# A two-layer graph network on one core: an earlier-reading first part, transfers of 128 rows, and the first layer's one-hot on ScalarE

## The chip, the core and the metric

The program runs on one core of a Trainium2 chip. Five engines work side by side and meet only at semaphores: TensorE (PE in the profile; its weight loads are PEld), VectorE (DVE), ScalarE (ACT), GpSimd (POOL) and SyncE (SP, which only issues transfers). ACT and POOL issue transfers too. Each engine takes its instructions strictly in the order in which they are written. The metric is device time in microseconds, and lower is better.

## The reference

Two message-passing layers over 12,500 nodes of 160 features (64 scalars and 32 vectors of three) and 200,000 edges. Cut to what matters:

```python
edge_index = stack([src, dst])                 # dst is sorted, src is not
for layer in (0, 1):
    xj   = x[dst]                              # gather, one row per edge
    msg  = tensor_product(xj, edge_attr) + linear(xj)      # 160 values per edge
    agg  = segment_sum(msg, src, num_segments=12500)       # scatter-add by src
    upd  = tensor_product(x, agg) + linear(x)  # bilinear: u, v -> w, 64*64*64 and more
    x    = layernorm(x + (x + upd))
return x
```

The first tensor product is linear in `xj` once the four edge attributes are given; the second is bilinear in the node's features and its sum.

## The kernel before, in words

**Tiles.** The nodes are cut into 100 tiles of `HM` = 125. The edges, in the order of `dst`, are cut into 98 chunks of 16 blocks of 128, and each chunk into two units of 8 blocks (196 units). For each node a row of 5 x 160 values (`table`) is stored in memory, from which every message of an edge that reads the node is a combination. A unit reads windows of 25 nodes of the table (`win`), builds a picking matrix for its edges (`pick_e`, on DVE, `select`), turns it on PE (`turn_pick`, into `s_ps`), ACT copies it out (`pick_out`), PE multiplies it with the window (`messages`, into `m_ps` and in the first part also `node_ps`), ACT copies the messages into `pay` (`pay_out`), and POOL writes them with eight indirect transfers a unit to the slots that belong to the edge's `src` tile (`scatter`). A node tile later reads its 17 x 128 slots (`msgs`), and PE sums them with a one-hot matrix of the slots' local node numbers (`onehot`, `sum_edges`).

**Three stages.** After a setup (loading and turning the edge lists, first tables) comes the first part, `chunk_sweep`: for each chunk layer 0's table tile eight ahead, both units of messages, and the sorting that gives each edge its slot. The sorting is `count` on PE (five small bf16 matmuls, twice a unit: `count(g, 0)` and `count(g, 1)`), `rank_unit` on DVE (a chain of 16 dependent operations that ends by raising `placed`) and the copy of the slot numbers on ACT. Then `step_sweep`, layer 0's node steps: step t sums the edges of tile t, runs the bilinear update of tile t - 1 (`bilinear(0)` to `(5)`, `turn_q`, `linear`), makes the layer-1 table rows of tile t - 2, and does chunk t - 7 of layer 1's messages. Last `node_sweep`, layer 1's node steps, with no messages. The middle of each sweep is a loop of two bodies on every engine.

**What sets the order.** Nothing but the order of the code on each engine, written out by hand, and the buffers: one `m_ps` and one `node_ps` bank, one `s_ps` bank, two `pick_n`, four `pay` and four `slot` buffers. In the first part `addressed` on ACT waits for `placed` of its own unit before it copies the slots, and `pay_out` of the same unit stands behind it. In a node step ACT begins with `where(0)`, `out(0, 0)` (the copy of `pick_n` for the first unit), `paid(0, 0)`, and ends with `turned_y` (copies of `ys_t`, `a_t`, `v_t`, for the next `bilinear(0)`) and `paid(1, 3)`; PE's step begins `bilinear(0)`, `turn(0, 0)`, `bilinear(1)`, `message(0, 0)`, and ends `turn_y`, `message(1, 3)`.

**The one-hot.** In layer 0 DVE makes it with one comparison over 128 x 2125, as the last thing of its step, for the next tile. In layer 1 ACT makes it: 17 `Square` activations of (node number - local number), a wait, and one `Relu(1 - 2 x)` over 128 x 2125.

**Transfers.** `slots` are cleared ahead of the scatter by ACT (`fill`, 22 rows of each of the 100 tiles per chunk, source one row of zeros 168 wide), and `spill_sums` by `clear`, once in two chunks. SP stores tables and results in 125 rows, and loads `x`, `spill_sums` in 125 rows and the windows in 125 (`WROWS` = 5 x 25).

Of the kernel before, what the change touches and what calls it, by code (L numbers as in the profile page):

```python
# [6 lines left out]
ALU = mybir.AluOpType  # L7
# [6 lines left out]
P = 128  # L14
# [3 lines left out]
HM = 125  # L18
# [60 lines left out]
def build(nc, x, src, dst, attr, weights, out):  # L79
# [35 lines left out]
    table = [nc.dram_tensor(f"table{layer}", [EDGE + N + EDGE, CHANNELS * D], F32).ap() for layer in range(2)]  # L115
# [4 lines left out]
    with ExitStack() as whole:  # L120
# [26 lines left out]
        zero = sb("zero", [P, ROW])  # L147
# [175 lines left out]
        def fill_ranks(eng, layer, r0, ranks, filled):  # L323

            rows = slots[layer][0:SLOTS, :].rearrange("(t r) c -> t r c", r=CAP)
            eng.dma_start(rows[:, r0:r0 + ranks, :] if isinstance(r0, int) else rows[:, bass.ds(r0, ranks), :],
                          zero[0:NT, :].unsqueeze(1).broadcast_to([NT, ranks, ROW])).then_inc(filled, 16)

        @block.sync
        def _(sp):  # L330
# [18 lines left out]

            def load_table_x(k):  # L350
# [3 lines left out]
                sp.dma_start(tx[b][0:HM, :], x[bass.ds(m * HM, HM), :]).then_inc(tx_in[b], 16)  # L354
# [52 lines left out]
            def load_windows(layer, k):  # L407
# [3 lines left out]
                if isinstance(c, int):  # L411
                    for m in (last_tile(c) - 1, last_tile(c)):
                        if m >= 0:
                            sp.wait_ge(s["t_stored"][m % 2], 16 * (m // 2) + 16)
                else:
                    sp.wait_ge(s["t_stored"][0], 16 * (ck + (1 if cb == 0 else 2)) + 16)
                    carry()
                    sp.wait_ge(s["t_stored"][1], 16 * (ck + 1) + 16)
                    carry()
                for hh in range(2):  # L420
# [4 lines left out]
                    for p in range(QUADS):  # L425
                        rows = table[layer][bass.ds(at[p], EDGE + WIN), :]
                        both = bass.AP(rows.tensor, rows.offset, [[D, WROWS], [EDGE * CHANNELS * D, 2], [1, D]], runtime_checks=rows.runtime_checks)
                        sp.dma_start(win[q][0:WROWS, 2 * p:2 * p + 2, :], both).then_inc(s["win_in"][q], 16)  # L428

            def store_table(layer, k):  # L430
# [1080 lines left out]
```

## Time and profile before

| | us |
|---|---|
| median of three runs | 8602.44 (8588.28 to 8614.11) |
| profiled execution | 8569.22, its span 8567.5 |
| setup, to the first scatter | 215.87 |
| first part, first scatter to last | 215.87 to 2865.9 |
| layer 0's node steps and the tail of the scatters | 2892 to 6024 |
| layer 1's node steps | 6024 to 8567.5 |
| busy over the span: PE, DVE, POOL, ACT | 79%, 82%, 52%, 33% |
| mean granted TensorE clock | 0.875 |

Read it by stages, since the shares differ: in the first part no engine is busy for more than about 60%, in layer 0's node steps PE and DVE are both busy for 96 to 97%, in layer 1's steps DVE for 96%. Granted clock 1.0 is 2.4 GHz, and 0.5 is 1.2 GHz; a mean between them is a mix of stretches at the one and at the other. POOL's busy time leaves out some 0.30 us between two scatters, in which it prepares the next.

### The profile page before, as it was taken

The page shows a single profiled execution, that of the slowest core. Times are in us where ns is not written, and L with a number is a line of the kernel's source. Part 1 is how long each engine was busy: PE and PEld are TensorE (multiplying, and loading weights), DVE is VectorE, ACT ScalarE, POOL GpSimd, SP SyncE. Part 2 cuts the span into 40 slices and gives each one's busy share as a digit, 9 for nine tenths or more (in the row PEclk, how much of TensorE's full clock was granted, in tenths as well). Part 3 has the DMA queues.
Part 4 walks back from the last instruction along what each step waited for, and adds up shares of the span by engine and source line. Part 5 has one row for each costly group of instructions (what it writes and reads, how often), then busy time and mean ns, then how long its engine had stood idle before and what let it go on. Part 6 is the DMA issues. An engine that isn't in the chain of part 4 may idle for free.

```text
span 8567.5 us, 139797 instructions
## 1 busy us (share of the span) xinstructions
PE 6727.2 (79%) x38863; PEld 5022.4 (59%) x38863; DVE 6998.7 (82%) x9199; ACT 2869.7 (33%) x9562; POOL 4429.7 (52%) x3371
## 2 busy tenths in 40 slices
PE   2666656666566699999999999997788888888888
PEld 1444444444444467777777777775556566666665
DVE  2655555555556799999999999996899999999999
ACT  1222222222222123333333333333344444444443
POOL 0655555555556357777777777777222222222222
PEclk5777777777777799999999999998899999999999
DMA  5555555555555256666666666664221212121211
GB/s 144 160 159 155 156 154 161 157 157 155 160 159 144 83 162 186 186 185 188 187 188 188 188 186 186 185 188 124 75 71 65 70 64 71 64 71 64 71 64 50
DMA packets 984231, 1163.06 MB, mean 136 GB/s; under 512 B 74878, under 2 KB 878173, under 8 KB 958553
## 3 DMA queue, kind: packets, MB, share of 16 engines
q10 hardware_dynamic: 460746, 590.81, 23.3%
q0 software_dynamic: 154640, 281.49, 11.6%
q1 hardware_dynamic: 368767, 289.81, 11.5%
q8 instruction: 39, 0.64, 0.0%
q14 instruction: 39, 0.32, 0.0%
HBM read 480.47 MB, written 681.31 MB: 136 GB/s over the span
## 4 chain that ended last, share of the span: by engine, by line
PE 39%; DVE 23%; issue 12%; DMA 8%; SPq 8%; ACT 5%; ACTq 4%; DVEq 1%; POOL 0%; POOLq 0%
PE prods_ps L1105 7%; PE turn_ps L1129 7%; PE node_ps L1138 6%; PE m_ps L1042 6%; DMA table<-tab 6%; DVE work L898 4%; SPq L428 3%; PE s_ps L1025 3%; PE node_ps L1042 3%; DVE pick L757 2%; DVE pick L755 2%; DVE rank L758 2%; PE node_ps L1150 2%; ACTq L1218 2%; DVE upd L904 2%
## 5 line engine op out<-in xcount | busy, mean ns | idle before, releaser
L544 POOL DMA_INDIRECT slots<-pay,slot x3136 | 3273.3, 1044 | 1727.9 <-ACT pay L1295 931.7
L601 POOL TENSOR_TENSOR q<-xt,yv 125x3072 f32<-125x3072 f32 x200 | 1130.4, 5652 | 2298.4 <-PE turn_ps L1129 2270.9
L1042 PE MATMUL m_ps<-win,pick_n 125*128 125x160 f32 x4704 | 1068.5, 355 | 784.0 <-ACT pay L1295 769.9
L1106 PE MATMUL prods_ps<-w_bil,ys_t 64*125 64x512 f32 x2400 | 1465.7, 708 | 0.0
L1042 PEld LDWEIGHTS m_ps<-win,pick_n 125*128 125x128 f32 x4704 | 769.5, 213 | 1113.2 <-ACT pay L1295 894.9
L898 DVE TENSOR_TENSOR work<-prods_ps,yv 125x1024 f32<-125x1024 f32 x1200 | 1392.9, 1217 | 11.2
L904 DVE TENSOR_REDUCE upd<-work 125x48 f32<-125x3072 f32 x400 | 1341.3, 3353 | 13.6
L1129 PEld LDWEIGHTS turn_ps<-ident,q 125*128 125x128 f32 x9600 | 1110.4, 192 | 175.6 <-issue 153.0
L1129 PE MATMUL turn_ps<-ident,q 125*128 125x125 f32 x9600 | 1162.4, 278 | 16.6 <-ACT q_t L1373 16.4
L1105 PE MATMUL prods_ps<-w_bil,a_t 64*125 64x512 f32 x1600 | 1016.9, 741 | 176.1 <-ACT v_t L1402 115.2
L882 DVE TENSOR_TENSOR work<-prods_ps,xt 125x1024 f32<-125x1024 f32 x800 | 964.1, 1219 | 149.7 <-PE prods_ps L1106 135.0
L1138 PEld LDWEIGHTS node_ps<-msgs,onehot 128*125 128x125 f32 x6800 | 931.0, 188 | 169.0 <-issue 169.0
L1138 PE MATMUL node_ps<-msgs,onehot 128*125 128x160 f32 x6800 | 979.7, 303 | 17.6 <-ACT onehot L1449 11.0
L886 DVE TENSOR_REDUCE upd<-work 125x16 f32<-125x1024 f32 x800 | 950.8, 1209 | 0.0
L1025 PE MATMUL s_ps<-ident,pick_e 128*125 128x128 f32 x3136 | 646.2, 341 | 285.6 <-ACT pick_n L1277 276.8
L1025 PEld LDWEIGHTS s_ps<-ident,pick_e 128*125 128x125 f32 x3136 | 564.0, 247 | 377.6 <-issue 367.5
L754 DVE TENSOR_TENSOR before<-before,prods_ps 128x100 f32<-128x100 f32 x392 | 100.3, 256 | 830.1 <-PE prods_ps L1013 830.1
L1277 ACT COPY pick_n<-s_ps 125x512 f32<-125x512 f32 x784 | 459.7, 586 | 768.1 <-PE s_ps L1025 458.9
L1295 ACT COPY pay<-m_ps 128x320 f32<-128x320 f32 x1176 | 506.5, 431 | 483.9 <-PE m_ps L1042 475.2
L1105 PEld LDWEIGHTS prods_ps<-w_bil,a_t 64*125 64x125 f32 x1600 | 287.4, 214 | 594.3 <-DVE work L882 288.3
L1105 PE MATMUL prods_ps<-w_bil,ys_t 64*125 64x512 f32 x800 | 448.7, 641 | 109.8 <-DVE work L882 109.8
L1446 ACT ACTIVATE onehot<-node_iota,msgs 128x125 f32<-128x125 f32 x1700 | 503.9, 395 | 54.4 <-POOLq L588 54.4
(216 smaller groups left out, 8479.8 us busy)
## 6 DMA issues: line engine op xcount, KB each, us to landing
msgs<-slots ACTq DMA_DIRECT2D x200, 1428.0 KB, 6.5
slots<-zero ACTq DMA_DIRECT2D x183, 1443.8 KB
win<-table SPq DMA_DIRECT2D x784, 156.2 KB
table<-tab SPq DMA_DIRECT2D x200, 390.6 KB
slots<-pay,slot POOLq DMA_INDIRECT x3136, 5.5
spill_sums<-zero_rows ACTq DMA_DIRECT2D x88, 180.0 KB, 9.5
spill_in<-spill_sums SPq DMA_DIRECT2D x200, 78.1 KB
rec<-edge_recs SPq DMA_DIRECT2D x196, 64.0 KB, 8.6
```

Source lines behind the costliest of these rows:

```text
L544: g.indirect_dma_start(out=slots[layer][:, :], out_offset=bass.IndirectOffsetOnAxis(ap=slot[q][:, j:j + 1], axis=0), in_=pay[q][:, j, :], ...
L601: g.tensor_tensor(q3[0:HM, :].rearrange("p (i u v) -> p i u v", i=3, u=V), xt[nb][0:HM, S:D].rearrange("p (u i) -> p i u", i=3).unsqueeze( ...
L882: ve.tensor_tensor(third(r), prods_ps[r % 2][0:HM, :].rearrange("p (w u) -> p w u", u=S), X[:, 0:S].unsqueeze(1).broadcast_to([HM, ROUND / ...
L886: ve.tensor_reduce(upd[0:HM, ROUND // S * (r - 1):ROUND // S * r], third(r - 1), AX_X, ALU.add).then_inc(s["upd"], 1)
L898: ve.tensor_tensor(wk[:, i, :, :].rearrange("p w (h k) -> p h w k", h=2), prods_ps[r % 2][0:HM, :].rearrange("p (h w k) -> p h w k", h=2, ...
L904: ve.tensor_reduce(upd1[:, :, w0:w0 + ROUND // KV], wk, AX_X, ALU.add).then_inc(s["upd"], 1)
L1025: mm = te.transpose(s_ps[0:WROWS, P * j:P * j + P], pick_e[hh][:, UB // 2 * part + j, :, :].rearrange("p n c -> p (n c)"), ident[:, :])
L1042: mm = te.matmul(to[:, D * j:D * j + D], pick_n[hh][0:WROWS, P * (2 * p + j):P * (2 * p + j) + P], win[q][0:WROWS, p, :], start=True, stop ...
L1105: te.matmul(prods_ps[r % 2][0:HM, 0:512], upper, w.bil[0:S, 512 * r:512 * r + 512], start=True, stop=True)
L1106: te.matmul(prods_ps[r % 2][0:HM, 512:1024], ys_t[S:P, :], w.bil[S:P, 512 * r:512 * r + 512], start=True, stop=True).then_inc(s["prods"], 1)
L1129: mm = te.matmul(turn_ps[:, HM * j:HM * j + HM], q3[0:HM, o:o + P], idn, start=(i == 0), stop=(i == 2))
L1138: te.matmul(node_ps[0:HM, 0:D], onehot[:, j, :], msgs[b][:, j, 0:D], start=(j == 0), stop=False)
```

## The change

Three things are changed at once.

1. **The first part's order.** On PE `count(g, 1)` stands behind the first `turn_pick` of its unit, and `count` for half 0 of the next unit stands ahead of `messages` 2 of this one. On ACT `addressed` is cut in two: `located` (the local numbers, no wait for `placed`) stays, and `slotted` (the slot numbers) comes one unit later, behind `pay_out` 0. POOL's scatter waits for both.
2. **Transfers.** Loads of `x`, of spilled sums and of windows take 128 rows instead of 125 (tables get rows of padding for it). Stores of 125 rows are cut into 112 and 13. The clearing of the slots is cut into 96 tiles and 4, and its source is now 11 rows of zeros, so that one contiguous piece has 1848 values instead of 168. Semaphore counts follow.
3. **The first layer's one-hot** leaves DVE. ACT makes it as in layer 1, in both layers behind `paid(1, 3)`, the last thing of the step; the first one comes after the spill's end.

```diff
 def fill_ranks(eng, layer, r0, ranks, filled):
     rows = slots[layer][0:SLOTS, :].rearrange("(t r) c -> t r c", r=CAP)
-    eng.dma_start(rows[:, r0:r0 + ranks, :] if isinstance(r0, int) else rows[:, bass.ds(r0, ranks), :],
-                  zero[0:NT, :].unsqueeze(1).broadcast_to([NT, ranks, ROW])).then_inc(filled, 16)
+    halves = 2 - ranks % 2
+    cols = ranks // halves * ROW
+    for t0, t1 in ((0, NTP), (NTP, NT)):
+        to = rows[t0:t1, r0:r0 + ranks, :] if isinstance(r0, int) else rows[t0:t1, bass.ds(r0, ranks), :]
+        eng.dma_start(to.rearrange("t (a r) c -> t a (r c)", a=halves),
+                      zero[t0:t1, 0:cols].unsqueeze(1).broadcast_to([t1 - t0, halves, cols])).then_inc(filled, 16)
...
+def put_tile(to, r0, frm, done):
+    sp.dma_start(to[bass.ds(r0, PART), :], frm[0:PART, :]).then_inc(done, 16)
+    sp.dma_start(to[bass.ds(r0 + PART, HM - PART), :], frm[PART:HM, :]).then_inc(done, 16)
...
-    both = bass.AP(rows.tensor, rows.offset, [[D, WROWS], [EDGE * CHANNELS * D, 2], [1, D]], runtime_checks=rows.runtime_checks)
-    sp.dma_start(win[q][0:WROWS, 2 * p:2 * p + 2, :], both).then_inc(s["win_in"][q], 16)
+    both = bass.AP(rows.tensor, rows.offset, [[D, P], [EDGE * CHANNELS * D, 2], [1, D]], runtime_checks=rows.runtime_checks)
+    sp.dma_start(win[q][:, 2 * p:2 * p + 2, :], both).then_inc(s["win_in"][q], 16)
...
@@ tensor engine, first part, chunk(k), one unit @@
     turn_pick(0, k, hh, 0)
-    count(4 * c + 2 * hh, 0)
+    count(4 * c + 2 * hh + 1, 1)
     turn_pick(0, k, hh, 1)
-    count(4 * c + 2 * hh + 1, 1)
     messages(0, k, hh, 0, both)
...
+    if hh == 0 or within(c, 0, NCH - 1):
+        count(4 * c + 2 * hh + 2, 0)
     messages(0, k, hh, 2, both)
...
@@ scalar engine, first part, chunk(k), one unit @@
     pick_out(0, k, hh, 1)
-    addressed(0, k, hh)
+    located(0, k, hh)
     pay_out(0, k, hh, 0, both)
+    if hh == 1 or within(c, 1, NCH):
+        slotted(0, k if hh else earlier(k), 1 - hh)
...
@@ scalar engine, end of node_step @@
     turned_y()
-    if layer == 1 and within(t, 0, NT - 1):
-        one_hot(later(k))
     paid(1, 3)
+    if within(t, 0, NT - 1):
+        one_hot(layer, later(k))
...
@@ vector engine, end of node_step @@
-    if layer == 0 and within(t, 0, NT - 1):
-        one_hot(later(k))
```

PE in the loop of the first part, first unit of a body, **before**; `prods_ps` is the bank of `count`, the two rows to `s_ps` are `turn_pick`:

```order
L1025 MATMUL s_ps<-ident,pick_e 125x128 [waits pick_out_l0,picked_l0]
...
L1011 MATMUL prods_ps<-bucket_onehot,after_bf 128x500 [waits hot]
...
L1025 MATMUL s_ps<-ident,pick_e 125x128 [waits pick_out_l0,picked_l0]
...
L1011 MATMUL prods_ps<-bucket_onehot,after_bf 128x500 [waits hot]
...
L1042 MATMUL m_ps<-win,pick_n 128x160 [waits pay_out_l0]
...
L1042 MATMUL node_ps<-win,pick_n 128x160 [waits pay_out_l0]
...
L985 MATMUL turn_ps<-ident,tx 96x125 [waits tx_in0]
...
L1042 MATMUL m_ps<-win,pick_n 128x160 [waits pay_out_l0]
...
L1042 MATMUL node_ps<-win,pick_n 128x160 [waits pay_out_l0]
```

The same place **now**:

```order
L1033 MATMUL s_ps<-ident,pick_e 125x128 [waits pick_out_l0,picked_l0]
...
L1019 MATMUL prods_ps<-bucket_onehot,after_bf 128x500 [waits hot]
...
L1033 MATMUL s_ps<-ident,pick_e 125x128 [waits pick_out_l0]
...
L1050 MATMUL m_ps<-win,pick_n 128x160 [waits pay_out_l0]
...
L1050 MATMUL node_ps<-win,pick_n 128x160 [waits pay_out_l0]
...
L993 MATMUL turn_ps<-ident,tx 96x125 [waits tx_in0]
...
L1019 MATMUL prods_ps<-bucket_onehot,after_bf 128x500 [waits hot]
...
L1050 MATMUL m_ps<-win,pick_n 128x160 [waits pay_out_l0]
...
L1050 MATMUL node_ps<-win,pick_n 128x160 [waits pay_out_l0]
```

The second count now is the one for the next unit, and it stands ahead of the two messages that wait for `pay_out` of this unit; the first is this unit's second half.

ACT at the same place **before** (`slot` and the second `pay` row are `addressed`, the rows to `pay` from a bank are `pay_out`):

```order
L1277 COPY pick_n<-s_ps 125x512 [waits pick_turned_l0]
L1284 ISA
L1286 REGISTER_ALU [waits placed]
L1287 ISA [waits scattered0_l0]
L1287 COPY slot<-slot_all 128x8
L1288 ISA
L1289 COPY pay<-rec 128x8 [waits rec_in0_l0]
L1294 REGISTER_ALU
L1295 COPY pay<-m_ps 128x2x160 [waits msg_l0]
...
L1295 COPY pay<-node_ps 128x2x160 [waits msg_l0]
```

and **now**:

```order
L1287 COPY pick_n<-s_ps 125x512 [waits pick_turned_l0]
L1294 REGISTER_ALU
L1295 ISA [waits scattered0_l0]
L1296 COPY pay<-rec 128x8 [waits rec_in0_l0]
L1308 REGISTER_ALU
L1309 COPY pay<-m_ps 128x2x160 [waits msg_l0]
L1302 ISA
L1303 ISA [waits placed]
L1303 COPY slot<-slot_all 128x8
...
L1309 COPY pay<-node_ps 128x2x160 [waits msg_l0]
```

The wait for `placed` moved behind the first copy of messages, and it is for the unit before.

ACT over the end of one layer-0 node step and the start of the next, **before**:

```order
L1402 COPY v_t<-turn_ps 96x125
L1295 COPY pay<-m_ps 128x2x160 [waits msg_l1]
L290 UNCONDITIONAL_BRANCH
L290 ISA
L1287 ISA [waits scattered0_l1]
L1287 COPY slot<-slot_all 128x8
L1288 ISA
L1289 COPY pay<-rec 128x8 [waits rec_in0_l1]
L1273 ISA
L1275 ISA [waits pick_turned_l1]
L1277 COPY pick_n<-s_ps 125x512 [waits msg_l1]
```

and **now**:

```order
L1420 COPY v_t<-turn_ps 96x125
L1309 COPY pay<-m_ps 128x2x160 [waits msg_l1]
L1464 ACTIVATE onehot<-node_iota,msgs 128x125 [waits edges_done_l0,msgs_in1_l0]
L1464 ACTIVATE onehot<-node_iota,msgs 128x125 x16
L1467 ACTIVATE onehot<-onehot,ones_f 128x2125 [waits squared]
L294 UNCONDITIONAL_BRANCH
L294 ISA
L1295 ISA [waits scattered0_l1]
L1296 COPY pay<-rec 128x8 [waits rec_in0_l1]
L1303 ISA
L1303 COPY slot<-slot_all 128x8
...
L1287 COPY pick_n<-s_ps 125x512 [waits msg_l1]
```

Eighteen activations now stand between the last `pay` copy of a step and the first `pick_n` copy of the next.

## Rows read from the trace of the kernel before

**Rows 1.** Engines by stage: window, busy us (instructions), granted clock, DMA share, GB/s

```profile
core 0: us, PE busy (x) PEld busy (x) DVE busy (x) ACT busy (x) POOL busy (x), PEclk, DMA share, GB/s
450.00:2800.00 2350.00, 1419.90 (x6355) 1115.33 (x6356) 1374.36 (x3619) 609.61 (x2046) 1365.53 (x1379) 0.73 0.56 156
3150.00:5856.00 2706.00, 2597.93 (x16520) 1959.24 (x16518) 2621.70 (x2413) 970.00 (x3493) 2096.97 (x1517) 1.00 0.64 186
6118.00:8500.00 2382.00, 2031.19 (x12357) 1447.18 (x12356) 2287.05 (x2078) 1016.30 (x3112) 514.55 (x94) 0.92 0.19 67
```

**Rows 2.** Waits in 450 to 2800: who waited for whom, us, times, longest

```profile
ACT slot L1287 <- DVEq L773: 961.2, 173, 6.3
DVE before L754 <- PE prods_ps L1013: 748.7, 212, 9.0
...
ACT pick_n L1277 <- issue: 287.5, 41, 10.3
```

**Rows 3.** Timeline, first part: start, us, engine, line, operation, idle before and its ender

```profile
2336.09 0.20 ACT L1287 COPY slot<-slot_all 128x8 int32 x1 [5.68 <-DVEq L773]
...
2336.77 1.43 PE L1042 MATMUL m_ps<-win,pick_n 125*128 125x160 f32 x4 [3.78 <-ACT pay L1295]
...
2340.02 5.63 ACTq L1218 DMA_DIRECT2D spill_sums<-zero_rows  x1
...
2345.84 2.22 ACTq L326 DMA_DIRECT2D slots<-zero  x1
...
2348.58 0.58 ACT L1277 COPY pick_n<-s_ps 125x512 f32<-125x512 f32 x1 [8.72 <-issue]
...
2351.78 0.26 DVE L754 TENSOR_TENSOR before<-before,prods_ps 128x100 f32<-128x100 f32 x1 [7.43 <-PE prods_ps L1013]
```

**Rows 4.** Groups of instructions, 450 to 2800: the scatters, busy, mean ns, idle before

```profile
L544 POOL DMA_INDIRECT slots<-pay,slot x1379 | 1366.5, 991 | 984.8 <-ACT pay L1295 684.5 <-issue 300.3
```

**Rows 5.** Timeline, POOL: the first and the last scatter of the first part

```profile
215.87 1.46 POOL L544 DMA_INDIRECT slots<-pay,slot  x1 [157.69 <-ACT pay L1295]
...
2864.94 0.96 POOL L544 DMA_INDIRECT slots<-pay,slot  x1 [0.30 <-issue]
```

**Rows 6.** Issue on SP's queue, ns min/median/max: windows (450 to 2800), records (120 to 2800)

```profile
L428 SPq DMA_DIRECT2D win<-table x347: 277/1363/10717, 446.5 to 2790.1; - x174
...
L404 SPq DMA_DIRECT2D rec<-edge_recs x97: 365/366/6085, 196.2 to 2785.4; - x97
```

**Rows 7.** The chain that ended last, in the setup: start, us, what

```profile
14.26 6.08 SPq L354
...
158.92 7.27 DMA tx<-x
```

**Rows 8.** Timeline of one layer-0 node step, its handovers between PE and ACT

```profile
4671.34 0.27 PE L1159 MATMUL turn_ps<-ident,yx 125*96 125x125 f32 x1
...
4672.25 0.43 ACT L1295 COPY pay<-m_ps 128x320 f32<-128x320 f32 x1
...
4674.36 0.58 ACT L1277 COPY pick_n<-s_ps 125x512 f32<-125x512 f32 x1 [1.48 <-PE s_ps L1025]
...
4675.23 0.81 PE L1042 MATMUL m_ps<-win,pick_n 125*128 125x160 f32 x4
...
4701.34 0.27 PE L1159 MATMUL turn_ps<-ident,yx 125*96 125x125 f32 x1
```

**Rows 9.** Waits in 3600 to 5800 (73 node steps)

```profile
DVE work L882 <- PE prods_ps L1106: 43.4, 86, 1.0
```

**Rows 10.** Timeline, DVE: the one-hot at the end of steps 6 and 98

```profile
3066.74 2.37 DVE L858 TENSOR_TENSOR onehot<-msgs,node_iota 128x2125 f32<-128x2125 f32 x1
...
5855.23 2.37 DVE L858 TENSOR_TENSOR onehot<-msgs,node_iota 128x2125 f32<-128x2125 f32 x1
```

**Rows 11.** Timeline, ACT in a layer-1 step: its one-hot

```profile
7200.71 5.04 ACT L1446 ACTIVATE onehot<-node_iota,msgs 128x125 f32<-128x125 f32 x17
7205.79 2.07 ACT L1449 ACTIVATE onehot<-onehot,ones_f 128x2125 f32<-128x2125 f32 x1
```

More of the change, by code:

```diff
@@ L41 @@
 STRIP = 22
+HALF = STRIP // 2
 AHEAD = 5
+PART = 112
+NTP = 96
 LAG = 7
@@ L348, in _, with rows_of @@
             load_piece(so.src_i[1], so.dst_i[1], so.attr[1], 1, 1, piece_in[1])
+            def rows_of(t):
+                return P if within(t, 0, NT - 1) else HM
+            def put_tile(to, r0, frm, done):
+                sp.dma_start(to[bass.ds(r0, PART), :], frm[0:PART, :]).then_inc(done, 16)
+                sp.dma_start(to[bass.ds(r0 + PART, HM - PART), :], frm[PART:HM, :]).then_inc(done, 16)
             def load_table_x(k):
@@ L537, in scatter @@
                 g.wait_ge(s["located"], 2 * c + hh + 1)
+                g.wait_ge(s["slotted"], 2 * c + hh + 1)
                 if within(c, 2 - 2 * layer, STRIPS[layer]):
-                    g.wait_ge(s["filled"][cb], 16 * ck + 16 * layer)
+                    g.wait_ge(s["filled"][cb], 32 * ck + 32 * layer)
                 for p in range(PAIRS):
@@ L850, in spill @@
                 ve.wait_ge(s["sp_done"], 1)
-            def one_hot(k):
-                t, half, b = k
-                s = LS[0]
-                ve.wait_ge(s["msgs_in"][b], 16 * half + 16)
-                if within(t, 1, NT):
-                    ve.wait_ge(s["edges_done"], t)
-                ve.tensor_tensor(onehot[:, :, :], msgs[b][:, :, LOCAL:LOCAL + 1].broadcast_to([P, BLOCKS, HM]),
-                                 node_iota[:, :].unsqueeze(1).broadcast_to([P, BLOCKS, HM]), ALU.is_equal).then_inc(s["hot"], 1)
             def node_step(layer, k, chunk):
@@ L930, in normalise @@
                 if within(n, 2, NT):
-                    ve.wait_ge(s["stored"][b], 16 * half)
+                    ve.wait_ge(s["stored"][b], 32 * half)
                     if layer == 0:
@@ L1066, in _ @@
                     first_table((m, m // 2, m % 2), part)
+            count(0, 0)
             chunk_sweep(te, chunk)
@@ L1210, in fill @@
                 if within(c, 4 - 2 * layer, NCH):
-                    ac.wait_ge(filled, 16 * ck - 16 + 16 * layer)
+                    ac.wait_ge(filled, 32 * ck - 32 + 32 * layer)
                 fill_ranks(ac, layer, r0, min(STRIP, CAP - r0) if isinstance(c, int) else STRIP, filled)
@@ L1277, in pick_out, with located, slotted @@
                 ac.copy(pick_n[hh][0:WROWS, o:o + UB // 2 * P], s_ps[0:WROWS, 0:UB // 2 * P]).then_inc(s["pick_out"], 1)
-            def addressed(layer, k, hh):
+            def located(layer, k, hh):
                 c, ck, cb = k
                 s, q = LS[layer], 2 * cb + hh
+                if within(c, 2, NCH):
+                    ac.wait_ge(s["scattered"][q], 16 * UB * ck)
+                ac.wait_ge(s["rec_in"][cb], 16 * ck + 16)
+                ac.copy(pay[q][:, :, LOCAL:LOCAL + 1], rec[cb][:, UB * hh:UB * hh + UB, LOC:LOC + 1]).then_inc(s["located"], 1)
+            def slotted(layer, k, hh):
+                c, ck, cb = k
                 if layer == 0:
                     ac.wait_ge(placed, 2 * c + hh + 1)
-                if within(c, 2, NCH):
-                    ac.wait_ge(s["scattered"][q], 16 * UB * ck)
-                ac.copy(slot[q][:, :], slot_all[:, bass.ds(2 * UB * c + UB * hh, UB)])
-                ac.wait_ge(s["rec_in"][cb], 16 * ck + 16)
-                ac.copy(pay[q][:, :, LOCAL:LOCAL + 1], rec[cb][:, UB * hh:UB * hh + UB, LOC:LOC + 1]).then_inc(s["located"], 1)
+                ac.copy(slot[2 * cb + hh][:, :], slot_all[:, bass.ds(2 * UB * c + UB * hh, UB)]).then_inc(LS[layer]["slotted"], 1)
             def pay_out(layer, k, hh, p, banks):
@@ L1326, in _ @@
             chunk_sweep(ac, chunk)
+            slotted(0, (NCH - 1, NCH // 2 - 1, 1), 1)
             def deviation(layer, n):
@@ L1351, in where @@
                     if units:
-                        addressed(1, chunk, hh)
+                        located(1, chunk, hh)
+                        slotted(1, chunk, hh)
                 def features():
@@ L1460, in _ @@
             ac.wait_ge(LS[0]["sp_done"], 1)
+            one_hot(0, (0, 0, 0))
             step_sweep(ac, lambda k, chunk: node_step(0, k, chunk))
```

55 lines of the change are left out of this document (28 added, 27 removed).

## The prediction

> **What bounds the kernel now.** I read the engines by stage first, then in each stage the waits, the timeline of one period, and the queue's issue times.
>
> By stage [rows 1] the reader is to see two quite different stages. In 450 to 2800 (the first part) PE and DVE are busy for 60% and 58%, the granted clock is 0.73. In 3150 to 5856 (layer 0's node steps) PE is busy for 96% and DVE for 97% at clock 1.0. In layer 1's steps DVE is busy for 96%.
>
> *First part.* The window holds 1379 scatters, so 172.4 units of 8, a unit each 13.6 us. The waits [rows 2] form a ring: ACT waits for `placed` (961 us), DVE for PE's counts (749 us). The timeline [rows 3] shows why: `slot` ends a wait of 5.68 us, only then is `pay` copied, only then can PE go on (3.78 us idle), and PE's next count stands behind that. Beside the ring, once in a loop body (41 times, 7.0 us each) ACT stands in the issue of its own transfers (5.63 and 2.22 us), and DVE then waits 7.43 us. From the first to the last scatter the stage takes 215.87 to 2865.9 [rows 5], 2650 us, 13.52 us for each of the 196 units.
>
> *Layer 0's node steps.* From step 6's one-hot to step 98's [rows 10] are 92 steps in 2788.5 us, 30.3 us each. Both PE and DVE are full, so it matters who waits. DVE waits for PE's products 86 times, 43 us in 73 steps [rows 9]; no wait of PE for DVE stands among the long ones there, and one undisturbed step measures 4671.34 to 4701.34, 30.0 us, on PE's last transpose [rows 8]. I read PE's stream, with its short handovers to ACT, as the limit.
>
> **The change part by part.**
>
> *Order of the first part.* The ring is cut: messages no longer wait for this unit's `placed`, and the next unit's first count is ahead of them. What is late next is the busiest engine by itself. DVE: 13.63 less 749/172.4 = 4.34 is 9.3 us a unit. PE: 1420/172.4 = 8.2 us, at a clock of 0.73. POOL: 0.99 us a scatter [rows 4] and 0.30 between two [rows 5], so 8 x 1.30 = 10.4 us. POOL is the longest; four `pay` buffers let ACT run ahead of it. I take 10.6, with 0.2 for the waits at a unit's start; the lower end is 10.3, the upper is unknown, since an undiscovered second ring can hold anything up to the present 13.5, and I keep 12.0 for the range. 196 x (13.52 - 10.6) = 572 us saved. The first scatter waits half a unit more for `slotted`: 7 us.
>
> *Transfers.* ACT's 7.0 us a body are counted in the 572 already; they must go for it. A clearing DMA goes from 2200 pieces of 672 bytes to 200 of 7392. An issue of a window takes 1.36 us in the middle and up to 10.7, one of the records, which have 128 partitions, 0.37 in the middle [rows 6]: 125-row issues stand in a full queue. The Trainium skill ("DMA: Bandwidth & Descriptors", section "Why a DMA increments its semaphore by 16 and not by 1") says that a hardware-queue transfer is spread over the largest number up to 16 that divides its outer size: 5 for 125 rows, 10 for 100, all 16 for 128, 112 and 96. By that rule the queue was full because a third of the engines carried it, and the stall goes; if only the amount of bytes filled it, the stall stays, since the bytes do. The rows agree with the rule so far. Cost of the added issues (the 13-row and 4-tile ones): 0.3 us each on SP and ACT, under slack in both stages. In the setup SP stood 6.08 us in one small load and 7.27 us for another to land [rows 7]; between nothing and 60 us can go from there, and I take 40, an estimate: several such landings follow one another there, and the weight loads stand behind the same queue. In layer 0's steps the transfers lie beside a full PE: 0.3 us a step at most (30.3 against 30.0).
>
> *The one-hot off DVE.* 2.37 us a step [rows 10]. In steps 7 to 98 PE is the limit, so DVE only idles: 0. In steps 0 to 6, without messages, up to 7 x 2.4 = 17; I take 15, less 5 for the first one-hot, which now takes 7.15 us before step 0. 10 saved.
>
> *The one-hot onto ACT.* 17 Squares take 5.04 us and the Relu ends 7.15 us after their start [rows 11]. It starts when the last `pay` is copied, 4672.68 [rows 8], and ends at 4679.8. Only then can ACT copy `slot` (0.2) and `pick_n` (0.58): ready at 4680.6. PE's `m_ps` stands behind that copy, and began at 4675.23. So PE is held by 5.4 us. From there to its last transpose (4675.23 to 4701.61) PE has 26.4 us of work in one piece, and what follows on ACT is again v_t, `pay` and the one-hot: the delay returns in every step and nothing takes it back. Behind `pick_n` on ACT stand all `pay` copies and the deviation, behind PE's message stand `bilinear(2)` to `(5)`, for which DVE waits; DVE's 27.6 us fit.
>
> The hole costs PE its clock too. In the first part four matmuls of `m_ps` took 1.43 us after 3.78 us idle [rows 3], and 0.81 us in a full step [rows 8]. Layer 1's steps (94 in 2382 us, 25.3 each) run at clock 0.92 [rows 1], so 0.16 of them, 4.1 us, at 1.2 GHz: up to 2.0 us lost where PE sets the pace. I take 1.8; the ends are 0 and 2.6. The Trainium skill ("TensorE: Matmul & The Clock Gate", section "HAM oscillation — how this bites in real kernels") says that each wait between bursts throttles the next one, and puts the penalty at half the throttled time; by it the step is 37.2, without it 35.4. The two m_ps rows agree with it.
>
> A step is 30.0 + 5.4 + 1.8 = 37.2 us, 6.9 more than 30.3, in 93 steps (7 to 99): 642 us lost. Layer 1's steps keep their order, and their one-hot its place: 0. The scatters' tail after step 99 is POOL's and stays.
>
> *Sum.* -572 + 7 - 40 - 10 + 642 = +27 us on the profiled 8569.2. The median of the runs lies 33 us above that execution; with the same distance after, 8602.4 + 27 = 8629.
>
> **The rivals.**
>
> *No clock loss.* If PE keeps 2.4 GHz through the hole, a step costs 35.4 and the loss is 93 x 5.1 = 474: 8629 - 168 = 8461, faster. For it: layer 1 has stretches at 2.4 GHz through shorter gaps; against it: the first part's rows after 3.78 us. It ends on the other side; it decides from 1.5 us a step downward.
>
> *A second ring in the first part.* The counts, the two single banks and `slotted` still tie DVE, PE and ACT together; at 1.2 GHz PE's own 8.2 us would become more. At 11.6 us a unit the gain is 376: 8825. For it: 4 of 5 us of the saving rest on nothing else appearing; against it: four buffers and DVE's 9.3. A queue that stays full has the same size: 7.0/4 = 1.75 us a unit, mostly hidden by POOL.
>
> *ACT's one-hot is hidden.* If PE had other work in the hole or the 1.48 us that ACT waited [rows 8] were more, the steps stay at 30: 8629 - 642 = 7987. Against it: PE's order is fixed.
>
> *The first part does not move.* If POOL's start, not the ring, paced it: 9200. Against it: its 685 us of waiting for `pay` [rows 4].
>
> **How the numbers follow.** The forecast 0.53, no clock loss 0.17, the second ring 0.22, the hidden one-hot 0.04, no gain 0.04. About 0.3% (26 us) is what a measurement of this kernel can tell from no change; the forecast, +27, lies on that line, and its own range is 8560 to 8710, from 10.4 to 10.9 us a unit and 36.6 to 37.6 us a step. Of its 0.53, 0.08 fall below -26, 0.22 within, 0.23 above. Faster: 0.17 + 0.04 + 0.08 = 0.29. Same: 0.22 + 0.02 from the neighbours = 0.24. Slower: 0.47. The range leaves out the last two cases and the far ends of the rings: 8455 to 8830.
>
> **What would show it.** The one-hot rows on ACT, 7.1 us in each layer-0 step, and behind them a PE wait at `m_ps` for ACT of 5 us or more; the distance of PE's last transposes near 37 us; the stage's clock below 1.0, near 0.92; DVE idle for 8 us in a step. In the first part scatters without gaps, 10.4 to 10.8 us a unit, DVE's wait for counts under 1.5 us a unit, ACT's wait for issue gone, window issues near 0.4 us. Wrong it is if the unit stays above 11.2 us, or if PE's wait at `m_ps` in the steps is under 4 us.

## The result and the profile after

The changed kernel takes 8634.0 us (median of 5 runs, 8627.95 to 8637.45). The kernel before, run beside it, takes 8595.9 (5 runs, 8569.8 to 8614.1). The ratio is 1.0046, with a 95% interval of 1.0025 to 1.0067: about 38 us slower. The forecast was 8629.

Two changes of 600 us stand behind that small number. Stage by stage, in the two profiled executions (8569.2 and 8637.4 us):

| stretch | before | after | difference | forecast |
|---|---|---|---|---|
| to the first scatter | 215.9 | 188.1 | -28 | -33 |
| first part, first to last scatter | 2649.1 | 2072.1 | -577 | -572 |
| from there to layer 0's step 7 | 225.4 | 232.3 | +7 | -10 |
| steps 7 to 99 | 2786.2 | 3453.5 | +667 | +642 |
| after step 99, the scatters' tail and layer 1 | 2691.0 | 2689.6 | -1 | 0 |

(The steps' places are POOL's products, one a step: 3090.4, 5876.6 before; 2492.6, 5946.1 after.) On the profiled executions that is +68 us, where the sum said +27. The medians differ by only 38: the profiled execution of before lies 27 us below the median of its five runs (and under the fastest of them, 8569.81), that of after 3 above its own. The forecast had added 33 us for the first of these distances and kept them for after. So the hit on 8629 owes 36 of the 41 us by which the sum was off to which executions were profiled, and that is luck; the two large terms are right to 1% and 4%.

By stage (columns as in [rows 1]):

```profile
450.00:2200.00 1750.00, 1169.67 (x6112) 916.33 (x6112) 1314.77 (x3488) 586.10 (x1957) 1346.60 (x1324) 0.82 0.67 200
2550.00:5900.00 3350.00, 2788.92 (x16511) 2092.85 (x16511) 2421.06 (x2323) 1575.52 (x5083) 1920.98 (x1520) 0.91 0.50 151
6200.00:8560.00 2360.00, 2019.36 (x12262) 1437.73 (x12262) 2267.45 (x2059) 1007.99 (x3094) 514.54 (x94) 0.92 0.20 68
```

In the first part every engine is busier than in [rows 1], POOL most: 1346.6 us and, beside it, the 0.30 us between scatters. In layer 0's steps PE fell from 96% to 83% and DVE from 97% to 72%: no engine is full any more, as when engines wait for each other in turn. Layer 1 is unchanged.

The first and last scatter of the first part, on POOL's timeline, answer to [rows 5]:

```profile
188.13 1.40 POOL L564 DMA_INDIRECT slots<-pay,slot  x1 [175.19 <-issue]
...
2260.26 0.96 POOL L564 DMA_INDIRECT slots<-pay,slot  x1 [0.30 <-issue]
```

The group of the scatters in 450 to 2200 answers to [rows 4]:

```profile
L564 POOL DMA_INDIRECT slots<-pay,slot x1324 | 1347.7, 1018 | 403.6 <-issue 366.4 <-ACT pay L1309 27.7 <-ACT slot L1303 5.5
```

The waits there answer to [rows 2]:

```profile
ACT pay L1296 <- DMA slots<-pay,slot: 542.4, 107, 7.8
POOL slots L564 <- issue: 366.4, 1202, 0.3
PE m_ps L1050 <- ACT pay L1309: 354.4, 91, 5.8
...
DVE before L774 <- PE prods_ps L1021: 211.1, 82, 5.8
```

2072.1 / 196 = 10.57 us a unit, and 8 x (1.018 + 0.30) = 10.54: POOL works without a pause, and its wait for `pay` went from 684.5 us in a window of 2350 [rows 4] to 27.7 in 1750. Now ACT waits for POOL's transfers to free a buffer of `pay` (542 us), and PE's waits at `m_ps` hang on that. Long waits of the two engines that feed POOL are therefore no loss: they are back pressure, that is, the waits of engines that are ahead of the one that sets the pace.

One layer-0 step of the changed kernel, its handovers between ACT and PE (compare [rows 8]):

```profile
4677.38 0.27 PE L1169 MATMUL turn_ps<-ident,yx 125*96 125x125 f32 x1
...
4678.69 5.04 ACT L1464 ACTIVATE onehot<-node_iota,msgs 128x125 f32<-128x125 f32 x17
...
4683.76 2.07 ACT L1467 ACTIVATE onehot<-onehot,ones_f 128x2125 f32<-128x2125 f32 x1
...
4685.93 0.57 ACT L1287 COPY pick_n<-s_ps 125x512 f32<-125x512 f32 x1
...
4686.64 1.43 PE L1050 MATMUL m_ps<-win,pick_n 125*128 125x160 f32 x4 [5.20 <-ACT pick_n L1287]
...
4699.38 4.88 PE L1148 MATMUL node_ps<-msgs,onehot 128*125 128x160 f32 x34
...
4714.91 0.27 PE L1169 MATMUL turn_ps<-ident,yx 125*96 125x125 f32 x1
```

The step takes 4677.38 to 4714.91, 37.53 us. PE stands 5.20 us at `m_ps`, behind `pick_n`, which stands behind the one-hot. After the hole four products of `m_ps` take 1.43 us, and from them to the node sums PE needs 12.74 us. In the kernel before the same stretch went from 4675.23 [rows 8] to

```profile
4685.88 4.88 PE L1138 MATMUL node_ps<-msgs,onehot 128*125 128x160 f32 x34
```

that is 10.65 us. 5.20 and 2.09 make 7.3 of the 7.5 us over the undisturbed 30.0. The 2.09 us stand in the first rows behind the hole, where PE has no gap: the granted clock of the 5.2 us from 4686.6 on is 0.51, that is 1.2 GHz, and it is 1.00 before the hole (4677.4 to 4681.4) and from 4691.8 on. Columns as in [rows 1]:

```profile
4686.60:4691.80 5.20, 5.17 (x16) 3.48 (x16) 0.00 (x0) 2.15 (x6) 1.92 (x2) 0.51 0.25 68
4691.80:4699.40 7.60, 7.60 (x47) 4.81 (x45) 7.36 (x9) 2.21 (x8) 5.92 (x6) 1.00 0.56 161
```

PE's waits over steps 9 to 97 hold nothing else of the hole's size:

```profile
PE m_ps L1050 <- ACT pick_n L1287: 468.0, 89, 5.3
```

Four of the runs below (the hole filled with 22 products, six scatters, both on the clearing) ran on another chip than the rest, where the kernel before itself took 9657.5 us and engines of the first part stood up to 17 us for "issue" and up to 14 for "remote", so their times compare only with each other and with that figure.

### The profile page after: what moved, and what is told of

Same layout as the page of the kernel before. It is cut to its first block, busy times and chain, and to the rows that moved or that the text cites. A ratio compares the mean times of both kernels' runs of the same rounds, so it can differ in the third digit from the quotient of the medians.

```text
span 8635.7 us, 143679 instructions
## 1 busy us (share of the span) xinstructions
PE 6699.2 (78%) x38863; PEld 4979.0 (58%) x38863; DVE 6762.7 (78%) x9099; ACT 3556.5 (41%) x11362; POOL 4286.4 (50%) x3378
## 4 chain that ended last, share of the span: by engine, by line
PE 45%; issue 15%; ACT 11%; DVE 11%; POOL 10%; DMA 7%; ACTq 1%; SPq 1%; DVEq 0%; POOLq 0%
PE turn_ps L1139 10%; POOL slots L564 9%; PE prods_ps L1115 9%; PE node_ps L1148 9%; PE m_ps L1050 7%; DMA slots<-pay,slot 6%; ACT onehot L1464 5%; DVE work L909 3%; PE node_ps L1160 3%; DVE work L893 2%; PE s_ps L1033 2%; DVE upd L915 2%; DVE upd L897 1%; ACT q_t L1391 1%; ACT pay L1309 1%
## 5 line engine op out<-in xcount | busy, mean ns | idle before, releaser
L564 POOL DMA_INDIRECT slots<-pay,slot x3136 | 3127.2, 997 | 1455.9 <-issue 1036.4
L1050 PE MATMUL m_ps<-win,pick_n 125*128 125x160 f32 x4704 | 1104.9, 366 | 900.5 <-ACT pick_n L1287 495.8
L1116 PE MATMUL prods_ps<-w_bil,ys_t 64*125 64x512 f32 x2400 | 1548.5, 746 | 0.0
L1050 PEld LDWEIGHTS m_ps<-win,pick_n 125*128 125x128 f32 x4704 | 826.4, 227 | 1243.3 <-issue 755.9
L1115 PE MATMUL prods_ps<-w_bil,a_t 64*125 64x512 f32 x1600 | 1100.2, 798 | 166.4 <-ACT v_t L1420 120.2
L1464 ACT ACTIVATE onehot<-node_iota,msgs 128x125 f32<-128x125 f32 x3400 | 1008.0, 396 | 118.3 <-POOLq L608 118.3
L1033 PE MATMUL s_ps<-ident,pick_e 128*125 128x128 f32 x3136 | 613.0, 328 | 114.4 <-ACT pick_n L1287 111.8
L1391 ACT COPY q_t<-turn_ps 128x500 f32<-128x500 f32 x400 | 230.1, 575 | 1057.4 <-PE turn_ps L1139 1057.4
L1115 PEld LDWEIGHTS prods_ps<-w_bil,a_t 64*125 64x125 f32 x1600 | 308.9, 230 | 604.8 <-issue 299.2
L1033 PEld LDWEIGHTS s_ps<-ident,pick_e 128*125 128x125 f32 x3136 | 526.2, 232 | 209.0 <-issue 111.5
L1115 PE MATMUL prods_ps<-w_bil,ys_t 64*125 64x512 f32 x800 | 448.1, 640 | 114.8 <-DVE work L893 114.8
```

Of the source, the lines that this page charges most:

```text
L564: g.indirect_dma_start(out=slots[layer][:, :], out_offset=bass.IndirectOffsetOnAxis(ap=slot[q][:, j:j + 1], axis=0), in_=pay[q][:, j, :], ...
L1033: mm = te.transpose(s_ps[0:WROWS, P * j:P * j + P], pick_e[hh][:, UB // 2 * part + j, :, :].rearrange("p n c -> p (n c)"), ident[:, :])
L1050: mm = te.matmul(to[:, D * j:D * j + D], pick_n[hh][0:WROWS, P * (2 * p + j):P * (2 * p + j) + P], win[q][0:WROWS, p, :], start=True, stop ...
L1115: te.matmul(prods_ps[r % 2][0:HM, 0:512], upper, w.bil[0:S, 512 * r:512 * r + 512], start=True, stop=True)
L1116: te.matmul(prods_ps[r % 2][0:HM, 512:1024], ys_t[S:P, :], w.bil[S:P, 512 * r:512 * r + 512], start=True, stop=True).then_inc(s["prods"], 1)
L1464: last = ac.activation(onehot[:, j, :], node_iota[:, :], ACT.Square, bias=msgs[b][:, j, LOCAL:LOCAL + 1], scale=-1.0)
```

## The experiments

Times are medians of three rounds; ratios are to the kernel before, run beside each.

### The one-hot back on VectorE

```diff
 # the changed kernel
+                if layer == 0 and within(t, 0, NT - 1):
+                    one_hot(later(k))        # on VectorE, as before
```

> The changed kernel with layer 0's one-hot put back on VectorE at the end of its step (ScalarE makes it in layer 1 only, as before). Theory: the ScalarE one-hot costs all of the step's growth, 37.5 against 30.0 to 30.3 us, in 93 steps, since PE at the first m_ps of a step is queued behind it; the reordering and the transfers alone leave 10.6 us a unit in the first part. So 8634 - 93 x 7.3 = 7955 us, steps of 30.0 to 30.3 us at clock 1.0, and no wait of PE at m_ps for ScalarE above 1 us. Rival 1: part of the longer step is the new transfers or the moved scatters, then the steps stay above 32 us and the time above 8130. Rival 2: VectorE's 2.4 us decide as soon as the steps are short again, then 8634 - 93 x 5.1 = 8160.

Measured: 7939.3 us (7937.0 to 7941.7) against 8594.2 for the kernel before beside it, ratio 0.9234 (0.9216 to 0.9251). Its engines in 3150 to 5000, columns as in [rows 1]:

```profile
3150.00:5000.00 1850.00, 1780.49 (x11342) 1342.30 (x11343) 1796.99 (x1660) 674.64 (x2397) 1450.71 (x1045) 1.00 0.62 189
```

Steps are 30.13 us apart at clock 1.0, a unit of the first part 10.53. The theory held and both rivals fell: all that the steps lost comes from the place of the one-hot. This version beats both kernels by over 650 us.

### Only the one-hot on ScalarE

```diff
 # the kernel before
-                if layer == 0 and within(t, 0, NT - 1): one_hot(later(k))    # VectorE
+                paid(1, 3)                                                   # ScalarE
+                if within(t, 0, NT - 1): one_hot(layer, later(k))
```

> The kernel before with the ScalarE one-hot of layer 0 alone, nothing else of the change. Theory: the first part stays at 13.5 us a unit, each of 93 steps goes from 30.3 to 37.3 to 37.6 us as in the changed kernel: 8596 + 93 x 7.2 = 9265 us. Rival: in the kernel before ScalarE waits 4.9 us for xt each step, so the one-hot is partly hidden there or the delay grows by the late transfers: 8930 (half hidden) or above 9350.

Measured: 9247.8 us (9240.2 to 9250.7), ratio 1.0756 (1.0736 to 1.0776). The steps are 37.54 us apart, as in the changed kernel, the units 13.51. So a step with the one-hot on ACT takes the same time with and without the other two parts. The loss is 654 us here and 695 from the other side (8634.0 less 7939.3). Of the difference, 15 us are the steps that are lost against: 30.28 us in the mean with the old transfers, 30.12 with the new ones. The other 26 are no more than what separates runs of the kernel before: its profiled execution lies 25 us below the median of the runs beside these.

### Only the order, only the transfers

```diff
 # order_only: the kernel before, with
+                    located(0, k, hh)
+                    pay_out(0, k, hh, 0, both)
+                    if hh == 1 or within(c, 1, NCH): slotted(0, k if hh else earlier(k), 1 - hh)
 # transfers_only: the kernel before, with put_tile, rows_of, 128-row windows and the new fill_ranks
```

> The kernel before with the reordered first part alone (located and slotted apart, the next count ahead of messages 2 and 3), transfers and one-hot as before. Theory: the ring is cut and POOL's 8 x 1.3 us become the limit, but ScalarE still stands 7 us once in a loop body in the issue of its own transfers; of those four pay buffers hide the greater part: about 11.2 us a unit, 8596 - 196 x 2.3 = 8145 us. Rival 1 (the stall is hidden entirely): 10.6 a unit, 8025. Rival 2 (the queue, not the ring, held the units): above 12.6 a unit, 8420 or more.

> The kernel before with the new transfers alone (128-, 112- and 96-row transfers, clearing in pieces of 7392 bytes), order and one-hot as before. Theory: the ring through slot and the counts stays, so a unit is as the undisturbed ones of the kernel before, 12.1 us, since only the stall of 5.8 us once in four units goes; setup 28 us shorter: 8596 - 196 x 1.4 - 28 = 8295 us. Rival 1 (the bytes fill the queue, not the form): within 30 us of 8596. Rival 2 (the transfers were all that held the first part): 10.6 a unit, 8000.

Measured: the order alone 8279.6 us (ratio 0.9632, 0.9611 to 0.9652), a unit 11.93 us; the transfers alone 8320.7 us (0.9670, 0.9649 to 0.9691), a unit 12.53. Against 8594.2 that is 315 and 274 us, together 588; both at once bring 655. The theory of the transfers missed by 26 us. That of the order was 135 us too hopeful: 11.93 us a unit lie about midway between its 11.2 and its second rival's 12.6. What it left out is a row of the order alone, SP's issues of the records in 450 to 2250 (ns min/median/max):

```profile
L404 SPq DMA_DIRECT2D rec<-edge_recs x75: 1477/3482/6924, 456.2 to 2247.0; - x75
```

and, in its waits, who stands behind them:

```profile
DVE pick_e L723 <- DMA rec<-edge_recs: 448.3, 72, 10.8
```

In the kernel before the same issue took 0.37 us in the middle [rows 6]. Now SP also stands in the windows' issues (median 1.88 us, up to 8.15), the records come late, and DVE waits for them 448 us. So the full queue and the ring cover for each other, and removing one shows the other. With the transfers alone the ring stands as it did (450 to 2200):

```profile
ACT slot L1306 <- DVEq L792: 759.0, 138, 6.0
```

### The hole filled

```diff
 # the changed kernel, PE, message(0, 0) of layer 1
+                    te.wait_ge(s["pay_out"], before)
+                    for j in range(32):      # 22 in the second
+                        te.matmul(to[:, 0:P], ident[:, :], ident[:, :], start=True, stop=True)
                     te.wait_ge(s["pick_out"], 4 * c + 2 * hh + p // 2 + 1)
```

> The changed kernel with 32 idle multiplications of ident by ident (128 columns, about 0.15 us each at 2.4 GHz, 4.8 us) on PE ahead of the wait for pick_n at each layer-0 step's message(0,0), into m_ps, which the real product overwrites; they fill the 5.3 us in which PE stands. Theory: the hole's second price is the clock (the stretch from m_ps to node_ps takes 12.7 us against 10.6); with PE kept busy it stays at 2.4 GHz, m_ps takes 0.8 us, and the step is 30.1 + 5.3 = 35.4 us: 8634 - 93 x 2.1 = 8439 us, granted clock of the stage 1.0. Rival: the 2.1 us are other waits behind ScalarE's late copies (pay, the deviation), then the step stays at 37.5 and the time at 8634.

Measured: 8620.7 us (8615.3 to 8622.9), ratio 1.0038 (1.0021 to 1.0055), steps 37.27. The time missed the theory; PE's timeline in one step says why:

```profile
4664.37 7.41 PE L1047 MATMUL m_ps<-ident 128*128 128x128 f32 x64
4671.62 0.71 PE L1055 MATMUL m_ps<-win,pick_n 125*128 125x160 f32 x4
...
4682.17 4.88 PE L1153 MATMUL node_ps<-msgs,onehot 128*125 128x160 f32 x34
```

The 32 products take 7.25 us, not 4.8, and end 2.1 us after `pick_n` is there (copied 4668.94 to 4669.51). But the stage's clock is 1.00 instead of 0.91, and from `m_ps` to the node sums PE needs 10.55 us instead of 12.74, so the 2.1 us behind the hole are gone with the low clock. By itself this run does not refute the rival of late copies, since here ACT is 2.1 us ahead of PE. The rival falls by the rows of the changed kernel, where the products themselves are longer and PE has no gap, and by the run with a shorter one-hot below, where PE waits for ACT as there and loses time behind the wait in few steps only.

> The changed kernel with 22 idle multiplications in the hole instead of 32, which took 7.25 us (0.227 each) and so outlasted the hole by 2.1 us. Theory: 22 take 5.0 us and end before pick_n is there; at clock 1.0 the step is 30.1 + 5.2 = 35.3 us, 8634 - 93 x 2.25 = 8425 us. Rival: the late copies on ScalarE cost the 2.1 us, not the clock: 37.3 us a step, 8615, as with 32.

Measured: 9583.6 us, ratio to the kernel before on that chip 0.9909 (0.9885 to 0.9932). As a time it decides nothing: on that chip PE stands 0.46 us again and again for "issue", within the 22 products too, so that they last 6.98 us and end 1.8 us after `pick_n` is there. The stretch behind `m_ps` is 10.55 us (4725.52 to 4736.07 in the step read), as with 32. That a step of 35.3 us comes out of it was not shown.

### A shorter one-hot

```diff
 # the changed kernel, ScalarE, layer 0, steps 1 to 99
-                for j in range(BLOCKS):      # 17
+                for j in range(8):
```

> The changed kernel in which ScalarE makes only 8 of layer 0's 17 one-hot blocks in steps 1 to 99 (8 Squares, Relu over 8 blocks; the other blocks keep what step 0 left, so the node sums are not the reference's). That takes 9 x 0.3 + 1.0 = 3.7 us off ScalarE in each step. Theory: the hold of PE is the one-hot's length less 1.85 us of slack, so it shrinks to 1.6 us; whether the clock falls behind so short a hole is open: 31.7 us a step and 8634 - 93 x 5.85 = 8090 us if it stays at 2.4 GHz, 33.8 and 8285 if the loss is as large as behind the long hole. Rival (the step is long for another reason than the hold): above 35 us a step, 8400 or more.

Measured: 8126.2 us (8125.4 to 8128.9), ratio 0.9462 (0.9426 to 0.9498). The timeline of PE in one of its steps:

```profile
4673.01 0.27 PE L1169 MATMUL turn_ps<-ident,yx 125*96 125x125 f32 x1
...
4678.72 0.81 PE L1050 MATMUL m_ps<-win,pick_n 125*128 125x160 f32 x4 [1.66 <-ACT pick_n L1287]
...
4704.90 0.27 PE L1169 MATMUL turn_ps<-ident,yx 125*96 125x125 f32 x1
```

The hold is 1.66 us where 1.6 was expected, `m_ps` takes 0.81 at once, and the step is 31.89: 30.1 and the hold, with no clock loss behind it. But this holds for 80 of the 92 steps. The other 12 take 33.2 to 33.5 us, though no hold is above 1.8 us. In one of them, two steps earlier, the first four products take 0.81 us, the second four 1.02 and the third 1.25, and the clock of 4615 to 4620 is 0.66:

```profile
4613.32 0.81 PE L1050 MATMUL m_ps<-win,pick_n 125*128 125x160 f32 x4 [1.66 <-ACT pick_n L1287]
...
4617.60 1.25 PE L1050 MATMUL m_ps<-win,pick_n 125*128 125x160 f32 x4
```

So the hold shrank by 3.5 us, from 5.20 to 1.66, as did the one-hot, from 7.14 us to 3.60. The price of the clock, 2.1 us in every step behind the long hole, was 1.6 us in one step of eight behind the short one.

### The one-hot in pieces, where ScalarE waits anyway

```diff
 # the changed kernel, ScalarE, layer 0
+ after load_msgs:            one_hot_piece(0, later(k), 0, 6)
+ after out(1, 0):            one_hot_piece(0, later(k), 6, 12)
+ after paid(0, 3), next step: one_hot_piece(0, k, 12, 17) and the Relu
```

> The changed kernel with layer 0's ScalarE one-hot in three pieces where ScalarE waits anyway: 6 Squares behind the copy of the node sums, 6 behind pick_out(1,0), 5 and the Relu in the next step behind pay(0,3), ahead of the features. Theory: nothing on PE waits for them, so a step is PE's own 30.0 us and VectorE is rid of 2.4 us: 8634 - 93 x 7.5 = 7935 us, no faster than with the one-hot on VectorE (7939), since PE and not VectorE sets the pace. Rival 1: the pieces delay q_t or the Relu comes later than PE's node sums (1 us of margin): 31 to 32 us a step, 8030 to 8120. Rival 2: VectorE was half of the limit, then the step falls below 29.8: under 7915.

Measured: 7949.7 us (7948.5 to 7953.5), ratio 0.9256 (0.9221 to 0.9291); steps 30.13 apart. Its engines in the same window:

```profile
3150.00:5000.00 1850.00, 1780.21 (x11359) 1344.47 (x11359) 1671.72 (x1598) 1098.22 (x3510) 1336.64 (x1042) 1.00 0.63 189
```

Here ACT makes the whole one-hot (424 us more work in these 61 steps than with it on VectorE), DVE has 125 us less, and PE's 1780 us of 1850 and the step are what they were. Where ACT waits anyway the 7.1 us cost nothing, and taking 2 us a step off a 97% busy DVE brings nothing, since PE sets the pace. Of the 11 us between this profiled execution and that of the version on VectorE, 5 lie in the first part and 4 between the last scatter and step 0, where the first one-hot takes ACT 7 us; the steps are equal.

### POOL as the first part's limit

```diff
 # the kernel with the one-hot on VectorE, the first part's scatters
-                        in_=pay[q][:, j, :]                     # 128 rows, j in 0..7
+                        in_=pay[q][0:64, j, :]                  # half_rows_scattered
+                        (j in 0..5 only, 128 rows)              # six_scatters
```

> The kernel with the one-hot on VectorE (7939 us) in which the first part's scatters move only partitions 0 to 63 of each payload, so that half of layer 0's messages are left out. Theory: the unit of 10.5 us is POOL's 8 x (1.02 + 0.30); a scatter of half the rows costs POOL less, the unit shrinks until VectorE's 9.3 us decide: about 9.6 us a unit, 7939 - 196 x 0.9 = 7760 us, with VectorE above 90% busy. Rival 1 (a second ring through the single banks and the counts sits just below POOL): the scatters get shorter but the unit stays above 10.2 us. Rival 2: the scatter's price doesn't depend on the rows, unit and time as they were, and this run tells nothing.

Measured: 7851.6 us (7849.7 to 7854.7), ratio 0.9141 (0.9106 to 0.9175). The group of its scatters in 450 to 2000, columns as in [rows 4]:

```profile
L565 POOL DMA_INDIRECT slots<-pay,slot x1224 | 1177.8, 962 | 373.1 <-issue 339.6 <-ACT pay L1322 32.0 <-ACT slot L1316 1.5
```

Half the rows cost POOL 0.962 us in the mean where all cost 1.013 (0.89 and 0.96 in the median): a scatter's price is nearly all fixed. The unit followed, 10.12 us against 8 x (0.962 + 0.30) = 10.10, which is 0.41 less than with all rows, as 8 x 0.051 is. The 9.6 that I expected did not come, since the scatter hardly shrank, and rival 1 isn't confirmed by it either: POOL was still the limit.

> The kernel with the one-hot on VectorE (7939 us) with 6 instead of 8 scatters in each unit of the first part; the last quarter of each unit's messages is left out. Theory: POOL's own cost is 6 x (1.02 + 0.30) = 7.9 us then, and what was next decides: VectorE's 9.3 us of work a unit with some waiting, 9.5: 7939 - 196 x 1.0 = 7740 us. Rival (a second ring sits just below POOL's 10.5): above 10.0 us a unit, 7835 or more.

Measured: 8936.2 us, ratio 0.9244 (0.9221 to 0.9267) to the kernel before on that chip. With all eight scatters a unit took 14.07 us there (the run with 22 products), with six it took 11.11, from the first and last scatter on POOL's timeline:

```profile
188.38 1.08 POOL L564 DMA_INDIRECT slots<-pay,slot  x1 [175.43 <-issue]
...
2366.39 0.96 POOL L564 DMA_INDIRECT slots<-pay,slot  x1 [0.30 <-issue]
```

A quarter fewer scatters made the unit 21% shorter. But POOL's own time, 8 x (1.01 + 0.30) = 10.5 us and 6 x (1.03 + 0.30) = 8.0, fills neither unit, so this run does not show POOL as the limit there, and neither its theory (9.5) nor its rival (above 10.0) can be read from a unit that is long for other reasons. Which bound is next below 10.1 us stays open: no undisturbed run went below it.

### The clearing as before, and in small pieces

```diff
 # the kernel with the one-hot on VectorE, fill_ranks
+            eng.dma_start(rows[:, r0:r0 + ranks, :], zero row broadcast)   # clearing_as_before: 100 rows
+            eng.dma_start(rows of 96 and of 4, zero row broadcast)         # clearing_small_pieces
```

> The kernel with the one-hot on VectorE (7939 us), the clearing again as one transfer of 100 rows in pieces of 672 bytes; the 128- and 112-row transfers stay. Theory: the clearing carries most of the queue's bytes and packets, so the stalls come back nearly whole: 11.7 us a unit (11.93 with the order alone) and 20 us of setup, 7939 + 196 x 1.2 + 20 = 8195 us, with a long wait of VectorE for the records. Rival (the 125-row windows and stores were what held SP's queue): 10.7 us a unit, under 7985.

> The kernel with the one-hot on VectorE (7939 us), the clearing split into 96 and 4 rows as in the changed kernel but in pieces of 672 bytes. Theory (how evenly a transfer spreads over the engines decides, not the size of its pieces): within 40 us of 7939, the unit 10.5 to 10.7 us. Rival (the piece size decides: 2200 descriptors to a transfer against 200): the unit near 11.7 us and the time near 8170.

Measured: 9404.1 us (ratio 0.9732) and 9559.0 us (0.9878) on the chip of the 9657.5. The times do not decide it: units are 13.99 and 14.23 us, and 14.07 with the new clearing on the same chip. The issue times on SP decide something else, and against my theory. The windows' issues in 450 to 2250, ns min/median/max as in [rows 6], in the kernel before:

```profile
L428 SPq DMA_DIRECT2D win<-table x263: 305/1517/10717, 446.5 to 2243.5; - x132
```

With the order alone:

```profile
L428 SPq DMA_DIRECT2D win<-table x298: 305/1876/8147, 451.0 to 2244.2; - x149
```

With the transfers alone:

```profile
L446 SPq DMA_DIRECT2D win<-table x284: 372/376/583, 453.1 to 2228.7; - x142
```

With both and the clearing as before:

```profile
L442 SPq DMA_DIRECT2D win<-table x252: 2/373/1107, 472.1 to 2225.0; - x126
```

With 128-row windows an issue takes 0.37 us, also where the clearing is as before and a unit (14.0 us) about as long as in the kernel before (13.5). I had taken the clearing for the cause, as it carries most of the bytes; the rows put it on the form of the transfers on SP's queue (windows, stores and loads, which no run separates). A transfer that never changed its form shows it too: the clears of `spill_sums` on ACT have 96 rows in every kernel, and most of ACT's stall stood in their issue [rows 3]. Before, with the transfers alone, and with the clearing as before:

```profile
L1218 ACTq DMA_DIRECT2D spill_sums<-zero_rows x66: 338/1526/6755, 466.8 to 2229.7; - x66
...
L1237 ACTq DMA_DIRECT2D spill_sums<-zero_rows x72: 333/361/417, 476.4 to 2249.1; - x72
...
L1236 ACTq DMA_DIRECT2D spill_sums<-zero_rows x64: 338/368/2714, 463.4 to 2220.3; - x64
```

Two things limit this. No run on that chip has windows of 125 rows, so the last comparison is across chips. And the clearing's old form was not free: the 13-row stores of tables took 1.91 us to issue in the middle with it and 0.39 with the new clearing, on the same chip. What it is worth in time stays open.

The Trainium skill ("DMA: Bandwidth & Descriptors", section "Why a DMA increments its semaphore by 16 and not by 1") has such a transfer carried by the largest number of engines up to 16 that divides its rows, so 5 for 125 rows and 16 for 128. The rows agree with it; how many engines carried a transfer isn't in the trace.

## Why the prediction was right

*What bounds the kernel.* Right. First part: a ring, not a busy engine; after the cut POOL, 10.57 us for 10.6. Layer 0's steps: PE. The pieces' run shows it, since DVE's relief brought nothing.

*Order and transfers.* -577 for -572. I counted ACT's stall as gone with the transfers, without a price of its own for each part. It went from 7.0 us each time to 2.4 (104 us in 43 times in 450 to 2200), which costs nothing behind a full POOL. The runs give 315 and 274 alone and 655 together, setup (28) included. "The upper is unknown, since an undiscovered second ring can hold anything" named the risk; such a ring was there (windows, records, DVE's wait), and only the transfers opened it. That the same change opened it was luck as far as the working goes: it did not foresee this ring. The rival of a second ring at 11.6 falls for the changed kernel, though it describes the order alone at 11.93.

*Setup.* -28 for -33 with the half unit.

*The one-hot off DVE.* Forecast -10, measured +7 between the last scatter and step 7. The 15 us from steps 0 to 6 did not come (step 0 to 7 took 188.1 before and 190.0 after, so DVE was not their limit), and the first one-hot costs 5 us. A term with the wrong sign, too small to matter.

*The one-hot onto ACT.* The mechanism as described, in place and order. Hold 5.2 to 5.3 us for 5.4; clock 2.1 for 1.8, inside its ends of 0 and 2.6; a step 37.5 for 37.2. From step 7 to step 99 there are 92 steps and not 93; 92 steps of 7.26 us are 667, where 93 of 6.9 made 642.

*The sum.* It was off by 41 us between the profiled executions and by 5 in the medians. Its own doubt, that a forecast of +27 lies on the line of what can be told apart, was fair: the measured +38 is above that line.

*The rivals.* No clock loss: refuted by the clock of 0.51 behind the hole and 1.43 us at `m_ps`; the filled hole shows the stretch that this rival assumed, 10.55 us. Hidden one-hot: false for this order, true for the pieces (7949.7, where the rival said 7987). First part unmoved: false.

## What to carry to other kernels

Before work is moved from a full engine to an idle one, look at what stands behind it on the idle one: ACT was busy a third of the time, and 7.1 us at the wrong place cost 7.4 us a step, at the right place nothing. A relief of the second-fullest engine is worth nothing until the fullest moves. And where two causes hold a stage, a change that removes one can look poor, since the other steps forward: try them together too.

## What the runs showed of the hardware

- An indirect scatter of 64 rows costs POOL 0.962 us and one of 128 rows 1.013, with 0.30 us between two in either case: here the number of scatters counts far more than their rows.
- A 5.2 us hole of PE in every step was followed by a stretch at 1.2 GHz (2.1 us lost; clock 0.51 over 5.2 us in the step read, 0.91 in the stage); behind a 1.66 us hole 12 steps of 92 lost 1.6 us (stage 0.99); with the hole filled by idle products the clock stayed at 1.00.
- A product of two 128 x 128 fp32 tiles stands in the trace as two, and takes 0.227 us; read from a row of four transposes I had taken it for 0.15.
- Issuing a 125-row window took 1.4 to 1.9 us in the middle and up to 10.7, a 128-row window 0.37 and at most 1.1. A 96-row transfer on ACT's queue, never changed itself, went from 1.5 us to 0.36 when the transfers beside it were changed.
